# A two-layer graph network kernel: three tiles' row sums moved from TensorE to ScalarE by a second load, and six row-sum chunks moved from VectorE to ScalarE

## The reference, cut to what matters

```python
# x: (8192, 128), adj: (8192, 8192), f32
adj_hat = adj + I
d = 1 / sqrt(sum(adj_hat, axis=1))
x1 = layernorm(x + relu((adj_hat * d[:, None] * d[None, :]) @ (x @ W) + b))
support = x1 @ weight
o = relu(support + adj @ support + x1 @ self_weight)
o = o - mean(o, axis=0); o = o / sqrt(mean(sum(o * o, axis=1) + 1e-6))
out = layernorm(x1 + o)
```

## Time and profile before

| | before |
|---|---|
| runs | 1857.39, 1858.1, 1862.03 us, median 1858.1 |
| profiled execution | 1858.79 us, span 1856.9 us |
| PE busy | 1656.4 us, 89% |
| DVE busy | 1450.6 us, 78% |
| ACT busy | 1202.0 us, 65% |
| HBM read | 566.49 MB |

### The profile page before, as it was taken

One profiled execution on the slowest core, in us unless ns is written; L12 is line 12 of the kernel. 1 busy time (PEld: TensorE's weight loads), 2 busy tenths in 40 slices (PEclk: granted clock), 3 DMA queues, 4 the chain that ended last, 5 costly groups with the idle time before them and its releaser, 6 DMA issues.

```text
span 1856.9 us, 20667 instructions
## 1 busy us (share of the span) xinstructions
PE 1656.4 (89%) x7682; PEld 1262.9 (68%) x7682; DVE 1450.6 (78%) x1893; ACT 1202.0 (65%) x1636; POOL 21.2 (1%) x42
## 2 busy tenths in 40 slices
PE   1078998989998999889999999999989999999993
PEld 0055565656565666667778888888868888877872
DVE  4476687797888889977767665665599999999997
ACT  3486696767766655645545554554568888888875
POOL 0000000000000000000000000000000000000001
PEclk7598999999999999999999999999999999999995
DMA  9999999999999668944445545545589999999943
GB/s 398 422 420 421 421 399 420 406 422 407 402 373 411 250 250 364 336 159 159 167 173 182 178 167 200 182 181 183 205 329 386 386 387 386 386 375 369 386 184 91
DMA packets 87460, 572.04 MB, mean 308 GB/s; under 512 B 8960, under 2 KB 17152, under 8 KB 19264
## 3 DMA queue, kind: packets, MB, share of 16 engines
q1 hardware_dynamic: 84928, 562.07, 76.8%
q0 software_dynamic: 2432, 8.65, 1.4%
HBM read 566.49 MB, written 4.19 MB: 307 GB/s over the span
## 4 chain that ended last, share of the span: by engine, by line
PE 61%; DVE 16%; DMA 15%; ACT 5%; issue 2%; SPq 1%; ACTq 0%; DVEq 0%
PE acc L1043 16%; PE acc L1045 15%; PE acc L1049 15%; DVE raw_low L735 6%; DMA s<-in_adjN 5%; DMA raw<-in_adjT 4%; DMA zr<-in_adjT 4%; ACT hi L561 3%; PE pC L1024 2%; DVE o_low L735 2%; DVE s L755 1%; DMA s<-in_adjT 1%; PE pA L1043 1%; DVE zr_low L735 1%; PE pA L1045 1%
## 5 line engine op out<-in xcount | busy, mean ns | idle before, releaser
L1043 PE MATMUL acc<-hi,rhi 128*128 128x512 f32 x1792 | 731.4, 408 | 77.7 <-DVE raw_low L735 51.6
L735 DVE TENSOR_TENSOR raw_low<-raw,hi 128x1024 fp32r<-128x1024 f32 x558 | 662.5, 1222 | 69.5 <-ACT hi L561 64.2
L561 ACT ACTIVATE hi<-raw 128x1024 fp32r<-128x1024 f32 x558 | 573.1, 1054 | 159.2 <-DMA raw<-in_adjT 75.6
L1045 PE MATMUL acc<-raw_low,rhi 128*128 128x512 f32 x1520 | 602.6, 396 | 0.0
L1049 PE MATMUL acc<-hi,rlo 128*128 128x512 f32 x1792 | 560.4, 394 | 0.0
L1043 PEld LDWEIGHTS acc<-hi,rhi 128*128 128x128 f32 x1792 | 341.8, 191 | 223.6 <-DVE raw_low L735 102.7
L1049 PEld LDWEIGHTS acc<-hi,rlo 128*128 128x128 f32 x1792 | 341.2, 190 | 74.4
L1045 PEld LDWEIGHTS acc<-raw_low,rhi 128*128 128x128 f32 x1520 | 291.1, 191 | 59.9 <-issue 3.1
L561 ACT ACTIVATE hi<-zr 128x1024 fp32r<-128x1024 f32 x158 | 164.4, 1057 | 43.3 <-PE acc L1049 19.1
L734 DVE TENSOR_TENSOR rlo<-zr,rhi 128x256 fp32r<-128x256 f32 x123 | 52.1, 424 | 170.8 <-ACT hi L561 170.7
L555 ACT ACTIVATE rhi<-zr 128x256 fp32r<-128x256 f32 x123 | 50.8, 413 | 193.4 <-PE acc L1049 193.4
(11 more groups left out here) (186 smaller groups left out, 1667.0 us busy)
## 6 DMA issues: line engine op xcount, KB each, us to landing
raw<-in_adjT SPq DMA_DIRECT2D x279, 1024.0 KB, 5.1
zr<-in_adjT SPq DMA_DIRECT2D x79, 1024.0 KB, 5.8
raw<-in_adjN SPq DMA_DIRECT2D x54, 1024.0 KB, 16.7
o<-in_adjT SPq DMA_DIRECT2D x32, 1024.0 KB, 12.5
s<-in_adjN SPq DMA_DIRECT2D x30, 1024.0 KB, 17.4
s<-in_adjT SPq DMA_DIRECT2D x30, 1024.0 KB, 15.0
zr<-in_adjN SPq DMA_DIRECT2D x28, 1024.0 KB, 19.4
s<-in_xT POOLq DMA_DIRECT2D x8, 512.0 KB, 4.4
```

Source lines behind the costliest of these rows:

```text
L561: S.activation(hi[n % DEEP][:, :], slice_of(chunk, j), ACT.Copy).then_inc(hi_ready, 1)
L735: V.tensor_sub(low_of(chunk, j), slice_of(chunk, j), hi[n % DEEP][:, :].bitcast(f32)).then_inc(slice_split, 1)
L1043: T.matmul(banks[h][:, :], a, hi[n % DEEP][:, part], start=opens, stop=False, skip_group_check=True)
L1045: T.matmul(banks[h][:, :], a, low_of(chunk, j)[:, part], start=False, stop=False, skip_group_check=True)
```

## The change

Three tiles, (6,4), (7,5) and (7,6), are no longer summed by TensorE. Each is loaded a second time in natural layout (4 MB each, four natural chunks) in the stage in which it is multiplied, 5, 6 and 7, and summed on ScalarE. Its multiply chunks are no longer `summed`. The natural chunks q = 3 of rows 4 to 6 (six chunks) go from VectorE to ScalarE. `rsum` gets one area per row block, since rows 6 and 7 now gather sums early, `degree` reduces row 7 as well, and GpSimd's first load of `x` waits for the last degree.

```diff
@@ planner
+    TWICE = {5: [(6, 4, q) for q in range(Q)], 6: [(7, 5, q) for q in range(Q)], 7: [(7, 6, q) for q in range(Q)]}
+    twice = sorted({(i, c) for blocks in TWICE.values() for i, c, _ in blocks})
...
-                sums.append(Chunk("sum", k, c, q, act=(q % 2 == 0 if k == 0 else q != 3), stage=k))
+                sums.append(Chunk("sum", k, c, q, act=(q % 2 == 0 if k == 0 else q != 3 or k >= NB // 2),
+                                  spot=c, stage=k))
+        sums += [Chunk("sum", i, c, q, act=True, spot=spot_of[i, c], stage=k) for i, c, q in TWICE.get(k, ())]
...
             multiply_block(products, i, k - 1, (L0,), new_visit(i, (L0,), 1, first=(k == 1)),
-                           summed=True, stage=k)
+                           summed=(i, k - 1) not in twice, stage=k)
...
-        rsum = [s1[:, 2 * BLK + r * NB * BG:2 * BLK + (r + 1) * NB * BG] for r in range(2)]
+        rsum = [s1[:, 2 * BLK + k * NB * BG:2 * BLK + (k + 1) * NB * BG] for k in range(NB)]
@@ gpsimd
             pool.wait_ge(sums_closed, NB)
+            pool.wait_ge(deg_ready, NB)
@@ degree
-                if k < NB - 1:
+                if first_spot[k] < NB:
```

More of the change, by code:

```diff
@@ L18 @@
     act: bool = False
+    spot: int = -1
     summed: bool = False
@@ L85, in graph_kernel @@
     EXTRA = {6: [(4, 5)], 7: [(5, 6), (2, 6)]}
+    TWICE = {5: [(6, 4, q) for q in range(Q)], 6: [(7, 5, q) for q in range(Q)], 7: [(7, 6, q) for q in range(Q)]}
+    twice = sorted({(i, c) for blocks in TWICE.values() for i, c, _ in blocks})
+    spot_of = {(i, c): i - [c2 for i2, c2 in twice if i2 == i].index(c) for i, c in twice}
+    first_spot = [k + 1 - sum(1 for i, _ in twice if i == k) for k in range(NB)]
     chunks = []
@@ L565, in sum_rows @@
                 for j in range(JB):
-                    g = chunk.col * BG + chunk.q * JB + j
+                    g = chunk.spot * BG + chunk.q * JB + j
                     ins = S.activation(slice_of(chunk, j), slice_of(chunk, j), ACT.Copy,
-                                       accum_out=rsum[chunk.row % 2][:, g:g + 1])
+                                       accum_out=rsum[chunk.row][:, g:g + 1])
                 ins.then_inc(act_summed, 1)
@@ L739, in sum_rows @@
                 dve.wait_ge(*landed(chunk))
-                g = chunk.col * BG + chunk.q * JB
-                V.tensor_reduce(rsum[chunk.row % 2][:, g:g + JB],
+                g = chunk.spot * BG + chunk.q * JB
+                V.tensor_reduce(rsum[chunk.row][:, g:g + JB],
                                 raw[chunk.buf].rearrange("p (g j) -> p g j", g=JB),
@@ L764, in degree @@
             def degree(k):
-                if k < NB - 1:
+                if first_spot[k] < NB:
                     dve.wait_ge(act_summed, act_sums_of[k])
                     dve.wait_ge(dve_summed, sum(1 for c in chunks if c.kind == "sum" and not c.act and c.stage <= k))
-                    V.tensor_reduce(own[:, :], rsum[k % 2][:, (k + 1) * BG:].rearrange("p (c g) -> p g c", g=BG),
+                    V.tensor_reduce(own[:, :], rsum[k][:, first_spot[k] * BG:].rearrange("p (c g) -> p g c", g=BG),
                                     AX.X, ALU.add).then_inc(deg_step, 1)
```

## The result

The changed kernel takes 1870.7 us (median of 6 runs, 1868.72 to 1873.8), the kernel before in the same measurements 1858.62. The ratio is 1.0062, 95% interval 1.0052 to 1.0072: slower, by about 12 us. The forecast was 1864.6 with a range of 1853 to 1875. The profiled execution has a span of 1866.9 us, 10.0 more than before; with 1868.72 us it is the fastest of its six, so about 2 us of the 12 are between executions and in no trace.

The account below looks back on a forecast made before the run. Transfers bound it to 600 us, then VectorE in cached and kept parts and TensorE in tails. +0.6 +5.4 -3.7 +5.6 -3.7 +2.3 = +6.5 us on the median 1858.1 gave 1864.6 us, range 1853 to 1875.

Parts of the forecast that it names:

- ScalarE's turn in front of every slice: ScalarE's in-order stream: a 2 us sum between two copies makes a chunk with a natural one beside it 4.3 us.
- Stage 4, +0.6: Three natural chunks go from VectorE to ScalarE in stage 4; together +0.6 us.
- Stage 5, +5.4: Stage 5 up to the split of (5,4,0): later landing and ScalarE's added sums put it at 582.7 against 577.30, +5.4 us.
- The pairs of (6,4), -3.7: Tails 0 to 7 of stage 5: TensorE no longer runs two pairs of row-sum matmuls, gaining 3.7 us.
- The clock I had named as a risk: TensorE's granted clock, 0.92 in 573 to 594: longer pauses could cost some us more; left out of the sum.
- Stage 6, cached part, +5.6: From the copy of (7,4,3) to the split of (6,5,0): 22.8 us in place of 17.2, +5.6 us.
- Stage 6, tails, -3.7 and +2.3: Stage 6 tails: -3.7 us without the pairs of (7,5); +2.3 us for ScalarE's natural chunks in tails 4 to 7.
- Stage 7, 0: Stage 7: no natural chunk added in its own slots, the pairs of (7,6) were hidden; 0.
- Carried to the end: Behind phase 1 the order is the same, so the +6.5 us was carried to the end.
- the first: Rival: ScalarE has room and the kernel is faster, -12 us, 1846; faster in all its sizes 0.12.
- the second: Rival: the two sides even out, half of +13.9 hides, -0.4 to +3 us, 1858 to 1861; chance 0.33.
- The third, transfers: Rival: transfers become the limit, twelve more MB, +15 us in place of ScalarE's cost in stage 6, 1873 to 1878; chance 0.15.

Follow-up runs that it names:

- experiment 3: Changed kernel, but ScalarE sums only 8 columns of each slice of (6,4), (7,5), (7,6), all loads kept: 1864.09 us, ratio 1.003.
- experiment 4: Changed kernel without the natural loads of (6,4), (7,5), (7,6); ScalarE does three copies on idle memory in place of each chunk: 1865.49 us, ratio 1.004.
- experiment 8: Changed kernel with stage 5's four kept chunks spread, one behind each of (5,4,0) to (5,4,3): 1867.49 us, ratio 1.0046.
- experiment 7: Changed kernel with TensorE also still summing (6,4), (7,5) and (7,6), so their row sums count twice: 1877.35 us, ratio 1.0107.
- experiment 6: Changed kernel with only tile (7,5) loaded twice, natural chunks q = 3 of rows 4 to 6 still on ScalarE: 1859.75 us, ratio 1.0009.
- experiment 1: Kernel before with the flag alone: natural chunks q = 3 of rows 4 to 6 summed on ScalarE, no tile loaded twice: 1859.19 us, ratio 1.0001.
- experiment 5: Changed kernel with only tile (6,4) loaded twice, natural chunks q = 3 of rows 4 to 6 still on ScalarE: 1863.48 us, ratio 1.0024.

## Why the prediction was nearly right, and where it was short

The direction and the largest term hold. The sum was +6.5; in the trace it is +8.9 at the end of phase 1 and +10.0 at the end, and +12 in the medians. The mechanism, ScalarE's turn in front of every slice, is shown in the cached part of stage 6: experiment 3 takes the cost away, experiment 4 keeps it. In stage 5 and in the tails of stage 6 landings would cost as much or nearly as much by themselves, so there it is one of two causes.

- *Stage 4, +0.6.* Measured -0.5 at (7,3,0); nothing that can be told.
- *Stage 5, +5.4.* 5.3 (-0.5 to +4.9 at (6,4,0)). It holds, but for two reasons at once: ScalarE's turn, as I had it, and landings, which alone would give 4.3 (-0.2 to +4.1, experiment 3). I had counted the full transfers there at nothing on top, which is right: with the loads gone it is +4.9 too (experiment 4).
- *The pairs of (6,4), -3.7.* Their worth is right (4.5 by experiment 7, with some clock in it). But the tails give only 1.5 (+4.9 to +3.4 at (5,5,0)). The missing step is the place of the kept chunks: the share rule put the last two of them in one slot, VectorE ran four adds in a row, TensorE paused and came back at a clock of 0.66. I had written "from here VectorE's chain with the kept chunks is as before". That sentence failed; putting the adds apart was worth 2.8 us (experiment 8). The clock I had named as a risk and left out. The kernel before has its own pause and a clock of 0.73 in that stage, but where VectorE holds TensorE anyway; the changed kernel has them where the tails begin and TensorE sets the pace.
- *Stage 6, cached part, +5.6.* 5.2 (+3.4 to +8.6), 5.2 alone (experiment 6). The 4.3 us a chunk was read from two rows of stage 5 and held to 0.02.
- *Stage 6, tails, -3.7 and +2.3.* Together -1.4; measured +0.2. This is the term that was mis-sized: the natural chunks of (7,6) cost 3.9, not 2.3. The 2.3 does not follow from its own figures: 17.8 us against 16.5 is 1.3. From the copy of (4,5,0) to that of the first cached chunk ScalarE took 18.9 us in the changed kernel (678.45 to 697.34). 16.9 of them were work, as I had added it up, and 2.0 were waits in place of 0.9: 1.4 for landings, 0.6 for TensorE. That is 2.4 over the 16.5. And the full -3.7 could not be had beside it: one of the two pairs, 2.0 us, runs inside this stretch, where TensorE no longer set the pace (experiment 6 has 1.7 up to (4,5,0) and 2.0 behind it). ScalarE in order of time in the changed kernel:

```profile
691.82 2.01 ACT L570 ACTIVATE hi<-raw 128x1024 fp32r<-128x1024 f32 x2 [0.29 <-DMA raw<-in_adjT]
694.94 1.06 ACT L576 ACTIVATE raw<-raw 128x1024 f32<-128x1024 f32 x1 [1.10 <-DMA raw<-in_adjN]
```

  The chain shows the transfer that the second of these waits for. It stands in SP's stream behind the load of (4,5,3), which goes out only when TensorE has multiplied (4,5,0):

```profile
687.41 7.51 DMA raw<-in_adjN
```

  With the loads gone (experiment 4) these tails cost 1.8 us less; with ScalarE's work gone and the loads kept (experiment 3) they cost as much as in the changed kernel. So the landings alone are enough here, and ScalarE's turn, which I had as the cause, is worth about half of them. TensorE's second pause, at 695, and the clock of 0.69 come behind this; they cost nothing more, since the difference stays at +8.8.
- *Stage 7, 0.* +8.8 at (6,6,0), +8.9 at (7,7,0). The pairs of (7,6) were hidden, as experiment 7 shows too.
- *Carried to the end.* +8.9 became +10.0 by steps of the clock in phase 2 (granted 0.77 from 800 to 810, where the kernel before has 0.88), which other kernels have with either sign.

So of the 6 us by which 1870.7 is over the forecast, 2.4 arose in phase 1, 1.1 in phase 2, and some 2 lie between executions, where the sum has nothing. Of the rivals, the first falls with experiments 1, 5 and 6, and the second with the result. The third, transfers, had a part of it right, the landings; its 1873 to 1878 does not follow from its own terms, which give 1872 to 1874.

The rule of the Trainium skill, Perfetto Trace Analysis, section Optimizing Scalar/DVE Operations, that a saturated VectorE may be relieved by ScalarE, gives nothing here: ratio 1.0001 with the flag alone. VectorE was saturated in the rows, but ScalarE's turn stands in front of the same splits.

## What to carry to other kernels

An engine that is busy 8 of 18 us may have no room if its stream is in order and each step of the pipeline needs it: ask how long the pipeline stands still for one more instruction between two of its turns, and compare that period (4.3 us here) with the other engines' (2.7). A chunk that is loaded and summed once more can cost by the engine's turn and by the landing: take each away by itself before a cost is put down to one of them. Where a planner's share rule places work, read the new order of all that it places, not only of what was added: four adds in a row cost 2.8 us of the 3.7 that a removed tile's sums gave. The gain was in that order: the same adds one place later and the close one chunk later, on top of a flag that changes nothing by itself, made the kernel 0.36% faster.

## What the runs showed of the hardware

- Row-sum matmuls of 32 columns in four column groups take 1.86 us a pair of chunks, where the sum of their durations is 9.6. Putting three tiles' pairs back cost 8.2 us; four of the six pairs are on the path, 7.4 us by the chain and 38 by the mean, so the price of the chain holds.
- The granted clock came back at 0.66 and 0.69 in the 5 us after two pauses of TensorE, and at 0.73 in the kernel before, after TensorE was busy 2.41 of 5 us; with the sums put back it was 0.50. These are means over 5 us, part at 2.4 and part at 1.2 GHz. The busy share then still reads 5.00 of 5, with x16 matmuls at 600 to 605 where the spread kernel has x22 at 599 to 604.
